# Projections stage: the order of VectorE's and ScalarE's work within a round is changed

## The reference, cut to what matters

```python
x = x + _layernorm(gated_attention(...))      # end of the third sublayer
n = _layernorm(x)                             # input of the fourth; kept (N4) for its residual
a = n * rsqrt(mean(n*n) + 1e-6)               # RMS norm; its weight is folded into wq, wk, wv
q = a @ wq.T                                  # 512 x 128 a batch
k = a @ wk.T                                  # 512 x 32
v = a @ wv.T                                  # 512 x 32
```

## Time and profile before

| what | value |
|---|---|
| median of three runs | 619.98 us |
| the profiled execution | 619.9 us |
| its span, first to last instruction | 618.2 us |
| TensorE busy | 511.6 us (83%) |
| VectorE busy | 483.3 us (78%) |
| ScalarE busy | 358.2 us (58%) |
| GpSimd busy | 238.5 us (39%) |
| mean granted TensorE clock | 0.876 of full speed |

### The profile page before, as it was taken

One profiled execution on the slowest core, in us unless ns is written; L12 is line 12 of the kernel. 1 busy time (PEld: TensorE's weight loads), 2 busy tenths in 40 slices (PEclk: granted clock), 3 DMA queues, 4 the chain that ended last, 5 costly groups with the idle time before them and its releaser, 6 DMA issues. The chain is left out here.

```text
span 618.2 us, 11394 instructions
## 1 busy us (share of the span) xinstructions
PE 511.6 (83%) x3652; PEld 277.1 (45%) x3652; DVE 483.3 (78%) x2079; ACT 358.2 (58%) x857; POOL 238.5 (39%) x463
## 2 busy tenths in 40 slices
PE   1967764789899967789999999999998898899871
PEld 1866664757766522122333333333333564465430
DVE  6899997666676678887999999999994255379786
ACT  3883345004356530036878888887878655566764
POOL 2000056530113331013555545455545344366674
PEclk9987775568989986557999999999999988999996
DMA  8000002000006842001111111111110000000001
GB/s 324 22 1 2 2 34 103 27 8 1 2 22 181 246 129 64 1 7 32 40 34 40 33 39 34 39 38 37 38 36 7 1 1 2 1 1 17 28 25 68
DMA packets 18874, 27.30 MB, mean 44 GB/s; under 512 B 3230, under 2 KB 14126, under 8 KB 18638
## 3 DMA queue, kind: packets, MB, share of 16 engines
q1 hardware_dynamic: 18174, 24.34, 13.2%
q10 hardware_dynamic: 576, 2.10, 0.9%
q0 software_dynamic: 64, 0.13, 0.1%
HBM read 14.11 MB, written 12.45 MB: 43 GB/s over the span
## 5 line engine op out<-in xcount | busy, mean ns | idle before, releaser
L1008 DVE CUSTOM_DVE_ANT_0 w_qkvT<-d_pS,w_qkvT 128x512 bf16<-128x512 f32 x480 | 203.9, 485 | 16.8 <-PE d_pS L999 11.9
L1678 ACT ACTIVATE d_P<-pT 128x768 f32<-128x768 f32 (+1 forms) x192 | 165.9, 882 | 62.7 <-PE pT L1704 61.0
L1558 POOL TENSOR_SCALAR_AFFINE_SELECT d_P<-d_P 128x256 f32<-128x256 f32 x256 | 102.6, 415 | 134.0 <-ACT d_P L1678 134.0
L999 PE MATMUL d_pS<-Ks,Qs 48*128 48x512 bf16 x480 | 97.9, 325 | 12.8 <-DVE hadamard L1008 8.9
L1704 PE MATMUL d_pO<-d_P,V 128*32 128x512 f32 (+3 forms) x1024 | 98.5, 460 | 1.4 <-POOL d_P L1558 0.9
L1704 PE MATMUL pT<-Qs,Ks 51*128 51x512 bf16 (+3 forms) x512 | 72.9, 312 | 2.0 <-ACT d_mT L1648 2.0
L999 PEld LDWEIGHTS d_pS<-Ks,Qs 48*128 48x128 bf16 x480 | 32.2, 96 | 55.9 <-DVE hadamard L1008 51.9
L1704 PEld LDWEIGHTS pT<-Qs,Ks 51*128 51x128 bf16 x512 | 20.7, 95 | 74.1 <-ACT d_P L1678 42.3
L487 POOL TENSOR_SCALAR N<-X,a_mv_s,a_rs 128x128 f32<-128x128 f32 x24 | 18.9, 797 | 80.9 <-DVE a_rs L331 80.9
L1008 DVE DVE_READ_ACCUMULATOR2_ANT hadamard<- 128x1 f32 x512 | 42.4, 83 | 0.0
L2021 ACT ACTIVATE e_T<-pT,comb 128x128 f32<-128x128 f32 x88 | 25.1, 381 | 23.0 <-issue 15.3
(11 more groups left out here) (345 smaller groups left out, 986.1 us busy)
## 6 DMA issues: line engine op xcount, KB each, us to landing
Qs<-q_stack SPq DMA_DIRECT2D x32, 192.0 KB, 3.1
q_stack<-Qp SPq DMA_DIRECT2D x8, 384.0 KB, 2.7
X<-in_x_dram ACTq DMA_DIRECT2D x4, 512.0 KB, 6.4
n_rows<-N SPq DMA_DIRECT2D x4, 512.0 KB, 2.9
q_stack<-Qp SPq DMA_DIRECT2D x8, 256.0 KB, 3.0
out_dram<-e_moe SPq DMA_DIRECT2D x8, 256.0 KB, 2.0
w_qkvT<-in_w_qkvT_dram SPq DMA_DIRECT2D x1, 1536.0 KB
Ks<-k_stack SPq DMA_DIRECT2D x32, 48.0 KB, 3.2
```

Source lines behind the costliest of these rows:

```text
L999: last = nc.tensor.matmul(dst[:, at:at + w], top.Qs[c][rows, h % 8, 128 * q:128 * q + 128], top.Ks[c][rows, h // 4 % 2, 0:w], start=True, ...
L1008: last = nc.vector.tensor_tensor_reduce(out=junk[:, at:at + w], in0=src[:, at:at + w], in1=top.wide_mask[:, 512 - w:512], scale=1.0, scala ...
L1558: last = nc.gpsimd.affine_select(out=view, in_=view, compare_op=ALU.is_ge, fill=0.0, base=0, pattern=[[0, 2], [1, 128]], channel_multiplie ...
L1678: nc.scalar.activation(P[pair % 4][:, :, P_AT[unit]:P_AT[unit] + w], pT[(3 * pair + unit) % 2][:, :, 0:w], ACT.Exp, scale=float(HD4) ** -0 ...
```

## The change

Within a turn, VectorE and ScalarE do the same steps in another order, and one of them a turn later or sooner. No instruction is added or taken away.

- VectorE: `rests` moves from the end of turn n+1 into turn n+2, behind `moments(n+2)` and ahead of `norm_scalars(n+2)`. For the last batch it stays where it was, behind fills 0 to 5. `normed(n)` moves from turn n+1 to the end of turn n, behind `norm_scalars(n)`.
- ScalarE: `second_part(turn-2)` moves from the first place of a turn to behind `deviations_x(turn)`; `by_channel(turn-1)` is then first.

```diff
                     if turn in batches:
                         attended(turn)
                         moments(turn)
-                    if turn - 1 in batches:
-                        normed(turn - 1)
+                    if turn - 2 in batches[:LAST]:
+                        rests(turn - 2)
                     if turn in batches:
                         norm_scalars(turn)
+                        normed(turn)
                     if turn - 1 == LAST:
                         maxima_ahead(0, 6)
-                    if turn - 1 in batches:
-                        rests(turn - 1)
-                    if turn - 1 == LAST:
+                        rests(LAST)
                         maxima_ahead(6, 8)
...
                 for turn in TURNS:
-                    if turn - 2 in batches:
-                        second_part(turn - 2)
                     if turn - 1 in batches:
                         by_channel(turn - 1)
                     if turn in batches:
                         deviations_x(turn)
+                    if turn - 2 in batches:
+                        second_part(turn - 2)
+                    if turn in batches:
                         normalise(turn)
                     if turn - 1 in batches:
                         first_parts(turn - 1)
```

## The result

The changed kernel takes 615.81 us (median of four runs, 615.12 to 616.1), against 620.06 for the kernel before on the same chip: a ratio of 0.9927, 95% interval 0.991 to 0.9944. The forecast was 615.2. The profiled execution took 615.88 with a span of 614.1, 4.1 less than before.

The account below looks back on a forecast made before the run. It took a chain through VectorE and ScalarE, 7.04 us a round, as the bound. Maxima 3.16 us sooner plus 1.59 of clock make 4.75, so 619.9 - 4.75 = 615.2; own range 614.4 to 617.0, overall 611.3 to 619.3.

Parts of the forecast that it names:

- The loop that set the pace: VectorE-ScalarE chain of 7.04 us a round; the change removes it, with VectorE's wait of up to 2.19 before K's rest.
- GpSimd's string: L1082 and L1085, run without a break, now meet `nb` and `normed` on VectorE; rounds 6.88 us against 7.04.
- `nb` falls at T + 1.43: T starts a rest of K; `nb`, 0.01 behind L1082, is held 2.12 us for the whole string, next turn T + 4.78.
- third case: Rival: no hold that matters on VectorE, TensorE's 6.27 sets the rounds, total 611.5; chance 0.11.
- The second case: Rival: hold for one GpSimd instruction only, `nb` let in before L1085, round 6.55, total 613.2; chance 0.20.
- The start: Turns 0 to 2: the extra `normed` is hidden, as turn 2 begins with V of batch 0.
- V0(2) = 181.12: Start of turn 2 on VectorE, at the V copy of batch 0, put at 181.12 us.
- the 3.16: End of the phase on VectorE: maxima begin at 223.8 instead of 226.96, 3.16 us sooner.
- The last projection at full clock: TensorE's idle gap before it shrinks to about 0.8 us, so it takes 2.91 instead of 4.50: 1.59 more gained.
- ScalarE's edit: ScalarE's copy to aT ahead of `second_part`; valued at nothing alone, since TensorE waits only 0.30 for aT.
- The clock of the next phase: Rival: TensorE's low-clock stretch in the next phase grows; 621.2 and more if by 12 us; chance 0.19, 0.10 slower.

Follow-up runs that it names:

- e4: Changed kernel with `normed` back in turn n+1, ahead of the rests; rests and ScalarE's order as changed: 612.76 us, ratio 0.9879 to the kernel before.
- e3: Kernel before with only `normed` moved to the end of its own turn; rests and ScalarE unchanged: 612.68 us, ratio 0.9849.
- e9: Changed kernel with two small unused reciprocals between VectorE's wait for the scalars and `nb`, to start `nb` behind L1082: 617.18 us, ratio 0.9953 to the kernel before.
- e10: Changed kernel in which GpSimd waits for its own L1082 before L1085, leaving a gap: 612.34 us, ratio 0.9858 to the kernel before.
- e1: Kernel before with ScalarE's reordering alone, `second_part` moved behind `deviations_x`: 625.26 us, ratio 1.0072.
- e7: Changed kernel with 12 more filler products on TensorE between the last batch's transposes and fill 2's score products: 613.13 us, ratio 0.9886 to the kernel before.
- e2: Changed kernel with ScalarE's old order, so VectorE's part alone: 635.35 us, ratio 1.0198 to the kernel before.
- e6: Changed kernel in which GpSimd waits for `normed` of the same turn before L1082: 610.05 us, ratio 0.9819 to the kernel before.
- e5: Changed kernel with one extra 128x8 reciprocal on VectorE ahead of the waits before `nb`: 615.62 us, ratio 0.9917 to the kernel before.
- e8: e4 with the last `normed` moved between fills 4 and 5: 613.41 us, ratio 0.9873 to the kernel before.
- e11: e6 without the 12 fillers ahead of the first score, and maxima of fills 0 and 1 ahead of batch 6's rests: 612.47 us, ratio 0.9867 to the kernel before.

## Why the prediction came out right, point by point

The total was 615.2 forecast and 615.8 measured. That it came so near is luck: three terms were off by 1.1 to 1.7 us each, and the errors nearly cancelled. That the change is faster, and by which loop, was foreseen.

- **The loop that set the pace**: right. No wait before the rest of K, and `normalise` no longer behind `normed`. e4 shows that moving the rests, with ScalarE's part, breaks the loop (rounds 6.17, no wait for the first part of K). Moving `normed` alone only shortens it (e3: rounds 6.53, the wait still 1.04).
- **GpSimd's string comes into the round**: right in kind. The step that failed is "`nb` falls at T + 1.43", 0.01 behind L1082. In five rounds it fell at T + 1.38 or T + 1.39, as the rest of Q started 0.57 behind that of K and not 0.61; L1082 came sooner too, by 0.03. In the sixth `nb` fell at T + 1.42. In all six it started in the same hundredth as L1082 or 0.01 ahead. So `nb` was free and `normed` took the hold, to T + 4.45 instead of T + 4.78. Rounds 6.57 instead of 6.88; turn 2 to the V copy of turn 8 took 39.61 us instead of 41.28: 1.67 better. e9 shows that the priced hold was right (2.12, round 6.85). The choice between held and free was a toss of 0.01 us. None of the prediction's cases had what then happened: its third case let `nb` win the tie and charged no hold at all, but with `nb` free it is `normed` that takes the hold.
- **The second case** (let in between L1082 and L1085) gave 6.55, near the measured 6.57, by a mechanism that did not act: the first `normed` was held through both (2184 ns). By e10 it acts if GpSimd pauses there. The Trainium skill ("SBUF — State Buffer", Who interferes with whom) has the ports held for the whole instruction. e1 and e10 agree for one instruction at a time (`nb` 1.14 beside an L1085 of 1.15; pieces of 1066 and 1179 ns); the trace after and e9 show holds over two GpSimd instructions that follow each other without a pause (2184 ns and 2.12 us).
- **The start**: "V0(2) = 181.12" was 182.18. TensorE's low-clock stretch at the start of the phase was 6.7 us and not 3.4, and the transposes and the first projection came later: 1.06 worse, though the phase itself began 0.3 sooner. I had carried the clock of the trace before over unchanged. With that clock the term was right: e10, which does the same up to there and had the 3.4 us, copies V of batch 0 12.83 us into the phase, and the prediction has 12.83 (181.12 less 168.29). The prediction's remark that "the start loses some" does not fit its own numbers: it had turn 2 at 181.12, 0.42 sooner than before (181.54), and the measured start is what lost. Nor was the held `normed` "most of" the 3.16: the rests of batch 6 take 1.2 in its place, so it is 1.9, beside 0.8 from the rounds and 0.4 from the start.
- **The last projection at full clock**: wrong. It took 4.5 instead of 2.9, and fill 5 came 4.84 behind its start instead of 3.30; as it began 0.23 sooner behind the first maximum, the term is 1.31 worse. I put TensorE's idle time ahead of it at 0.8; it was 2.43. With `nb` free, `a(7)` was there 2 us before I had it, and the last transposes started at 220.84 instead of near 223.0, while VectorE's first maximum came only 0.6 sooner. So the error on `nb` gave in the rounds and took at the end. e7 shows that the clock comes back when this idle time is filled, and that the price was right (1.61).
- **ScalarE's edit**, valued at nothing: wrong by itself. It costs 4.5 alone (e1), and without it VectorE's part costs 15 (e2). The prediction looked at whether TensorE waits for aT in the kernel before. It did not look at what else `second_part` releases, GpSimd's L1085 (e1), nor at what stands behind `second_part` once the rests come later, aT and the square roots (e2).
- **The clock of the next phase**, the slower rival: did not happen; from 249.04 and 244.99 to the end of the span both traces have 369.1 to 369.2 us.

Sum of the errors, in times of the whole trace: 615.2 - 1.67 + 1.06 + 1.31 = 615.9, and the profiled execution took 615.88. The errors of the terms add up to 4.0 us without their signs, that of the total is 0.7.

## What to carry to other kernels

When a step moves on one engine, list what starts on the other engines as a consequence, and lay those instructions beside the moved ones: a VectorE instruction that GpSimd can hold costs what GpSimd is doing then, and the order of starts, to hundredths of a microsecond, decides which one pays. A wait on the engine that has slack is a cheap way to keep such a string off a critical instruction (e6: one more wait on GpSimd, 4.3 us less in the phase than the change alone, 1.6 of it by the clock of the last projection). And an idle spell of TensorE ahead of a float32 product can cost twice, once as idle time and once in the clock of what follows (e7: 1.6 us).

## What the runs showed of the hardware

- A TENSOR_SCALAR of 128x128 from SBUF to SBUF and a SCALAR_TENSOR_TENSOR of 128x4 with both inputs in SBUF are held by GpSimd's TENSOR_TENSOR: 336 to 2184 ns and 0.16 to 2.12 us. Where two GpSimd instructions start without a pause between them, the hold spans both; a pause of 0.15 us lets VectorE in (e10).
- Near a tie the recorded starts do not settle who is held. `nb` in the same hundredth as L1082 or 0.01 ahead was free in six rounds of six (L1082 then took 1.18 instead of 1.15), and 0.15 or 0.16 behind it was held in all (e9). But the last `normed` was held for the whole string in the kernel before and in e1, though it started 0.02 ahead of L1082 (2415 and 2410 ns). Whether the kind of instruction makes the difference was not tried.
- TensorE's longest idle spell between the last batch's transposes and its projection, and the clock of that projection. Low (4.4 to 5.4 us): 5.05 (e1), 3.93 (before), 2.43 and 2.44 (changed), 2.35 (e5). Full (2.84 or 2.85 us): 0.37 and less (e2, e3, e6, e7). In between both happened: 1.14 (e8) and 1.74 (e9) full, 1.36 (e10), 1.33 (e11) and 1.64 (e4) low.
- An instruction ahead of a wait on the engine's own result can cost nothing (e5: a further reciprocal of 128x8, and `nb` still at T + 1.38 or 1.39).
